# Reordering the first loads, moving the gate arithmetic and waiting directly on row stores in a graph-attention kernel

## What is computed

```
h = relu(layernorm(x))                       # 8192 x 256
e = leaky_relu(h @ a[:256] + (h @ a[256:]).T, 0.2)
U = softmax(where(adj > 0, e, -9e15), axis=1)          # adj is 8192 x 8192
rowsum = sum(U * 0.5 * U, axis=1);  coe = sigmoid(temp)   # temp has 5 entries
feat = soft_threshold(U @ h + (1 - coe[2] - rowsum) * h)
out = x + coe[1] * feat_even2 + (1 - coe[1]) * (coe[0] * feat_odd2 + (1 - coe[0]) * h0)
```

## Time and profile before

| | |
|---|---|
| runs | 1456.39, 1456.82, 1457.94 us (median 1456.82) |
| profiled execution, its span | 1456.3 us |
| median over the span | 0.5 us |
| PE, DVE, ACT, POOL busy over the span | 62, 66, 59, 40% |
| DMA | 427.22 MB, mean 293 GB/s |
| first computation on x (DVE) | at 16.13 us |
| end of the preparation on DVE | at about 117 us |

### The profile page before, as it was taken

One profiled execution on the slowest core, in us unless ns is written; L12 is line 12 of the kernel. 1 busy time (PEld: TensorE's weight loads), 2 busy tenths in 40 slices (PEclk: granted clock), 3 DMA queues, 4 the chain that ended last, 5 costly groups with the idle time before them and its releaser, 6 DMA issues. The chain is left out here.

```text
span 1456.3 us, 27535 instructions
## 1 busy us (share of the span) xinstructions
PE 896.0 (62%) x3370; PEld 529.5 (36%) x3433; DVE 958.6 (66%) x5347; ACT 854.0 (59%) x1817; POOL 588.7 (40%) x644
## 2 busy tenths in 40 slices
PE   0013766777766767666776776776625655666676
PEld 0000244444443434333333433333314444544443
DVE  5887756768888877888888888887750122333444
ACT  3274576778888888888788788887230222121111
POOL 2002515444343233222212222221227777777775
PEclk9975678889999988998788778877656788788899
DMA  4879798789999999999999999997234566677886
GB/s 95 323 258 328 261 408 298 300 339 364 390 381 371 385 370 368 370 381 385 353 367 356 364 370 363 351 378 281 70 110 122 153 173 195 202 212 228 239 260 211
DMA packets 151277, 427.22 MB, mean 293 GB/s; under 512 B 30333, under 2 KB 112907, under 8 KB 134726
## 3 DMA queue, kind: packets, MB, share of 16 engines
q1 hardware_dynamic: 121084, 349.00, 64.5%
q0 software_dynamic: 30160, 77.90, 17.5%
HBM read 401.31 MB, written 33.90 MB: 299 GB/s over the span
## 5 line engine op out<-in xcount | busy, mean ns | idle before, releaser
L299 ACT ACTIVATE SG<-W,ABOVE 128x4096 bf16<-128x4096 f32 x126 | 466.9, 3706 | 64.8 <-DVE cnt L906 59.5
L587 POOL DMA_INDIRECT R<-haug_d,IDS x228 | 230.6, 1012 | 619.6 <-issue 619.6
L311 PE MATMUL TP<-SG,FOLD 128*128 128x512 bf16 x1004 | 308.2, 450 | 69.6 <-ACT SG L299 64.9
L629 ACT ACTIVATE DG<-ident,WSR 128x128 f32<-128x128 f32 x228 | 75.0, 391 | 312.0 <-PE ACC L643 289.6
L1528 DVE SCALAR_TENSOR_TENSOR W<-ACC,SELF,W 128x256 f32<-128x256 f32 x63 | 30.5, 484 | 241.3 <-PE ACC L643 241.2
L311 PEld LDWEIGHTS TP<-SG,FOLD 128*128 128x128 bf16 x1008 | 115.2, 123 | 182.4 <-ACT SG L299 65.9
L638 PE MATMUL ACC<-R,DG 128*128 128x256 f32 x538 | 180.7, 484 | 0.0
L637 PE MATMUL ACC<-XHO,ZB 128*128 128x256 bf16 x127 | 39.9, 314 | 204.3 <-DMA R<-feat_d,IDT 77.7
L638 PEld LDWEIGHTS ACC<-R,DG 128*128 128x128 f32 x538 | 119.6, 238 | 19.7 <-issue 0.3
L587 POOL DMA_INDIRECT R<-feat_d,IDR x115 | 110.3, 959 | 35.0 <-issue 33.8
L587 POOL DMA_INDIRECT W<-feat_d,IDR x113 | 107.5, 952 | 34.4 <-issue 33.2
(11 more groups left out here) (276 smaller groups left out, 2127.2 us busy)
## 6 DMA issues: line engine op xcount, KB each, us to landing
W<-in_adj_dram SPq DMA_DIRECT2D x128, 2048.0 KB, 10.3
haug_d<-R POOLq DMA_DIRECT2D x8, 1056.0 KB, 8.4
HTS<-haug_d SPq DMA_DIRECT2D x64, 132.0 KB
R<-in_x_dram SPq DMA_DIRECT2D x8, 1024.0 KB, 5.9
feat_d<-FTS SPq DMA_DIRECT2D x64, 128.0 KB, 1.7
W<-in_x_dram SPq DMA_DIRECT2D x64, 128.0 KB
W<-in_L_gnn_h_dram SPq DMA_DIRECT2D x64, 128.0 KB
W<-feat_d SPq DMA_DIRECT2D x64, 128.0 KB
```

The costliest lines, as they stand in the source:

```text
L299: nc.scalar.activation(SG[:, u, half(h)], W2[:, u, half(h)], ACT.Sign, scale=2.0 ** 100, bias=ABOVE[:], accum_out=DEG[:, u, h:h + 1]).then ...
L311: nc.tensor.matmul(KP[u], FOLD[:, b], SG[:, u, b * FW:(b + 1) * FW], start=False, stop=False)
L587: pool.indirect_dma_start(out=g[:, k, 0:w], out_offset=None, in_=table, in_offset=bass.IndirectOffsetOnAxis(ap=ids[:, k:k + 1], axis=0), * ...
L629: nc.scalar.mul(DG[:, u, k], ident[:], weights[:, k:k + 1])
```

## The change

The first two loads of x are issued at once, with no permit; a_row, temp_b and SELF follow behind the second. The semaphore of the small loads is split in two, `row_loaded` (DVE waits for it ahead of stats(1)) and `temp_loaded` (ACT waits for it ahead of the Exp). The Exp moves from ACT's first to ACT's last place in the preparation. The five gate instructions move into the next stage, behind `split_f2`. The three SELF instructions move from behind dots(0) to behind dots(2). `h_free` is gone: ACT waits on the semaphore of the store itself, and POOL's loop waits for no landing until both of its last stores.

```
         def prepare_sync(sp):
-            sp.dma_start(SELF[:], adj.rearrange(...)[0:N * N:N + 1]...).then_inc(diag_loaded, 16)
-            sp.dma_start(a_row[:], ...broadcast_to([P, 2 * F])).then_inc(consts_loaded, 16)
-            sp.dma_start(temp_b[:], ...broadcast_to([P, 5])).then_inc(consts_loaded, 16)
             for g in range(NG):
-                sp.wait_ge(x_free[g % 2], g // 2 + 1)
+                at_least(sp, x_free[g % 2], g // 2)
                 sp.dma_start(X[:, g % 2], x_g[g]).then_inc(x_loaded[g % 2], 16)
+                if g == 1:
+                    sp.dma_start(a_row[:], ...).then_inc(row_loaded, 16)
+                    sp.dma_start(temp_b[:], ...).then_inc(temp_loaded, 16)
+                    sp.dma_start(SELF[:], ...).then_inc(diag_loaded, 16)
...
         def prepare_gpsimd(pool):
-            for u in range(2):
-                pool.sem_inc(h_free[u], 1)
             with pool.Fori(0, NG // 2) as q:
                 for u in range(2):
                     pool.wait_ge(h_done[u], q + 1)
                     pool.dma_start(haug_g[...], H[:, u]).then_inc(h_stored[u], 16)
-                for u in range(2):
-                    pool.wait_ge(h_stored[u], 16 * q + 16)
-                    pool.sem_inc(h_free[u], 1)
+            for u in range(2):
+                pool.wait_ge(h_stored[u], 16 * (NG // 2))

         def prepare_scalar(act):
-            act.wait_ge(consts_loaded, 32)
-            nc.scalar.activation(coe[:], temp_b[:], ACT.Exp, scale=-1.0).then_inc(exp_made, 1)
-            for u in range(2):
-                act.sem_inc(x_free[u], 1)
             for g in range(NG):
...
                 act.wait_ge(norm_ready, g + 1)
-                act.wait_ge(h_free[u], g // 2 + 1)
+                at_least(act, h_stored[u], 16 * (g // 2))
...
+            act.wait_ge(temp_loaded, 16)
+            nc.scalar.activation(coe[:], temp_b[:], ACT.Exp, scale=-1.0).then_inc(exp_made, 1)
...
             norm(0)
-            dve.wait_ge(exp_made, 1)
-            step(nc.vector.tensor_scalar_add(one_m[:], coe[:], 1.0))
-            ...
+            dve.wait_ge(row_loaded, 16)
             for g in range(NG):
...
-                if g == 0:
+                if g == 2:
                     own = Steps(dve, self_step, 0, 2)
                     dve.wait_ge(diag_loaded, 16)
...
                 split_f2()
+                gates()          # the five instructions, behind a wait on exp_made
```

More of the change, by code:

```diff
@@ L252, in end @@
                 assert self.k == self.per, self.k
-        consts_loaded = sem("consts_loaded")
+        row_loaded = sem("row_loaded")
+        temp_loaded = sem("temp_loaded")
         ident_made = sem("ident_made")
@@ L265, in adj_preln_kernel @@
         h_stored = [sem(f"h_stored{u}") for u in range(2)]
-        h_free = [sem(f"h_free{u}") for u in range(2)]
         pads_set = sem("pads_set")
@@ L320, in prepare_sync @@
         def prepare_sync(sp):
-            sp.dma_start(SELF[:], adj.rearrange("a b -> (a b)")[0:N * N:N + 1].rearrange("(t p) -> p t", p=P), allow_slow_non_contiguous=True).then_inc(diag_loaded, 16)
-            sp.dma_start(a_row[:], a.rearrange("f one -> one f").broadcast_to([P, 2 * F])).then_inc(consts_loaded, 16)
-            sp.dma_start(temp_b[:], temp.rearrange("(one k) -> one k", one=1).broadcast_to([P, 5])).then_inc(consts_loaded, 16)
             for g in range(NG):
-                sp.wait_ge(x_free[g % 2], g // 2 + 1)
+                at_least(sp, x_free[g % 2], g // 2)
                 sp.dma_start(X[:, g % 2], x_g[g]).then_inc(x_loaded[g % 2], 16)
+                if g == 1:
+                    sp.dma_start(a_row[:], a.rearrange("f one -> one f").broadcast_to([P, 2 * F])).then_inc(row_loaded, 16)
+                    sp.dma_start(temp_b[:], temp.rearrange("(one k) -> one k", one=1).broadcast_to([P, 5])).then_inc(temp_loaded, 16)
+                    sp.dma_start(SELF[:], adj.rearrange("a b -> (a b)")[0:N * N:N + 1].rearrange("(t p) -> p t", p=P), allow_slow_non_contiguous=True).then_inc(diag_loaded, 16)
                 if g in (3, 4):
@@ L416, in prepare_vector @@
         def prepare_vector(dve):
-            step = Steps(dve, prep_step, 0, 4 + 10 * NG)
+            step = Steps(dve, prep_step, 0, 10 * NG)
             def stats(g):
@@ L1063, in body, with gates @@
                         C_.end()
-                top0 = Steps(dve, self_step, 6, 2)
+                top0 = Steps(dve, self_step, 10, 2)
+                def gates():
+                    step = Steps(dve, self_step, 6, 4)
+                    dve.wait_ge(exp_made, 1)
+                    step(nc.vector.tensor_scalar_add(one_m[:], coe[:], 1.0))
+                    step(nc.vector.reciprocal(coe[:], one_m[:]))
+                    step(nc.vector.tensor_scalar(one_m[:], coe[:], -1.0, 1.0, ALU.mult, ALU.add))
+                    nc.vector.tensor_tensor(one_c0[:, 0:1], one_m[:, 1:2], coe[:, 0:1], ALU.mult)
+                    step(nc.vector.tensor_tensor(one_c0[:, 1:2], one_m[:, 1:2], one_m[:, 0:1], ALU.mult))
+                    step.end()
                 def split_f2():
```

## The result

The changed kernel takes 1441.62 us, median of 4 runs (1438.67 to 1443.99), beside 1457.38 us (1456.39 to 1460.58) for the kernel before: ratio 0.9889 [0.9866, 0.9912]. Every ratio here is to runs of the kernel before on the same chip. Repeated beside more runs of the kernel before, the ratio was 0.9874 [0.9848, 0.9899] and 0.9876 [0.9855, 0.9896].

What follows compares the result with a forecast made beforehand. The prediction took DVE's chain in the preparation as the bound: 9.56 us from the head plus 1.8 us from gates and direct waits, 11.4 us in all, gave 1445.4 us, with 8 in 10 for 1442.5 to 1449.5.

Steps and rivals of the forecast that it cites:

- The head: Start of the preparation: x issued first at 0.97, so DVE starts at 6.57 instead of 16.13, 9.56 us off.
- The covers: Slack said to hide moved work: over 2 us for SELF instructions, 1.3 us for Exp, 2.6 us for gates.
- The vanished load: ACT's table load at line 741 in the next stage should vanish: counted as 0, with 1.3 us kept for the range.
- Gates off the head: Five gate instructions, 0.9 us, leave DVE between norm(0) and stats(1): at most 0.2 us gained, at dots(0).
- Direct waits on the stores: Relus in the preparation: about 0.1 us at relu(2), at most 0.1 at relu(4), 1.5 at relu(6); 1.8 with gates.
- the two meet, so 1.8 is also all there is: At dots(6), relu(6)'s end at 99.84 and stats(7)'s at 99.85 in the old clock cap the preparation's gain at 1.8 us.
- The later stages: Stages after the preparation were to keep their lengths within 1 us each.
- Only the head: Rival: store(4) lands later or store(5) did not hold h_free; gain 9.9 us, 1446.9 us; 12 in 100.
- the small loads in the way: Rival: a_row's load or SELF's transfers overlap x, costing 3.9 us on DVE's chain, 1449.3 us; 8 in 100.
- The loop gives it back: Rival: the sparse loop's 63 blocks lengthen, 0.18 us each cancelling the gain; 4 in 100 slower, 4 about as before.
- It doesn't do what it says: Rival: the first x is slow while instructions and first addresses are still fetched, so the head shrinks; no separate chance.
- More than the sum: Rival: the vanished table load counts for 1.3 us or the loop falls better, 1442 to 1444 us; 8 in 100.

Runs made afterwards that it cites:

- after_hfree: The changed kernel with h_free put back, POOL waiting for both landings at each turn's end and telling ACT: 1443.89 us, ratio 0.9911.
- before_x_first: The kernel before with only the loads of x first and without permits, everything else as it was: 1447.05 us, ratio 0.9930.
- before_unrolled: The kernel before with POOL's loop of four turns written out with fixed addresses, h_free and order kept: 1449.95 us, ratio 0.9969.
- relay kernel: The kernel before with h_free kept, but POOL telling of each store's landing before it takes up the next store: 1451.43 us, ratio 0.9971.
- the two on the other chip: The changed kernel with POOL's loop written out, without and with a 0.52 us fill on POOL ahead of stores (0) and (2): ratios 0.9851 and 0.9848.
- written out, with the fill: The changed kernel with POOL's loop written out and a 0.52 us memset on POOL ahead of stores (0) and (2): ratio 0.9848.
- after_again: The changed kernel run once more, unaltered, beside more runs of the kernel before: 1439.46 us, ratio 0.9874.

## Why the prediction was right and wrong

**The head was right.** 9.43 us of 9.56, with x issued at 0.97 and DVE 0.13 us later than said. Every kernel that has x first without SELF ahead shows it: statistics at 6.66 to 6.87, 7.10 with temp_b ahead. The small loads were not in the way: no idle time ahead of stats(1), and the next x, issued at 18.33, landed at 23.72.

**The covers held.** Dots(2) waited 4.76 us ("over 4.5"). The Exp is followed by 1.29 us of idle time, and the wait for PE behind the gates is 2.33 us, where 2.6 was said. Two table loads are left of three (0.97 and 99.74 us; before 0.97, 10.71 and 184.69). The load at 99.74 takes 1.28 us, the Exp starts 0.01 us behind its end and takes 0.21, so the two together are the 1.5 us of the working, and the copy of F2 was not held by them. The vanished load shows where I looked for it and is taken back where I said: 17.84 us of gain when the next Exp starts, 16.35 at the Sign behind it, which now waits 4.27 us for adj. Gates off the head gave 0.19 us for 0.2.

**The step that failed is "Direct waits on the stores".** It had 1.8 us with the gates, and for the waits alone the runs show 5.1 (kernel before) and 4.8 (kernel after). At F2's copy the sum is 3.6 us short, about what the median missed the forecast by (3.8). At relu(6) the working was right: on the landing of store(4), 74.17 + 8.3 = 82.47 against 82.57. At relu(4) the term was 0.1 us, because 61.92 + 11.2 = 73.12 and relu(4) came at 73.23. The wait was read rightly: in both profiles of the kernel before relu(4) stands on store(2)'s landing. What failed is that I carried the 11.2 us into the changed kernel as if they were the store's own. It lands in 8.4 to 9.0 us in all eight profiles with direct waits in the loop.

The second releaser I missed altogether. POOL took up store(3) at 72.23, and the `h_free` increments of the pair stand behind it:

```profile
72.23 0.89 POOL L380 DMA_DIRECT2D haug_d<-R  x1 [9.42 <-DVE F L461]
```

I had named exactly this for store(5) and relu(6), and did not ask it of store(3). In after_hfree, before_x_first and before_unrolled the store was down 1 to 3 us before, and relu(4) still came right behind store(3). The row that bounds the step was there: equal stores took from 9.0 us, and 61.92 + 9.0 is 70.9, 2.3 us ahead of 73.23. I used the landings' scatter to bound relu(6) from below and not relu(4) from above. With it the low end would have been about 1440.

A bound of the same step was wrong too, without harm to the sum: "the two meet, so 1.8 is also all there is" took DVE at dots(6) for the limit. Dots(6) did lose all its idle time, but the chain goes on from relu(6) over ACT to relu(7), and the copy of F2 had relu(6)'s whole gain.

**What it showed in its place.** Relu(4), 12.48 - 10.04 = 2.4 us more than relu(2): by the rows nearly all of it is store(2)'s landing, 8.9 us instead of 11.2. With direct waits POOL takes store(2) up 0.4 us ahead of the next load of x instead of 0.3; whether that tenth is the reason is the question of the table below. With `h_free` only 0.9 us of that could have been had, since relu(4) would then have stood on store(3) at 72.3; the rest needs the order. The relay kernel, with a landing of 9.1 us and relu(4) at 70.63, has both. Relu(6), 2.5 us more: 1.4 is the order that I had, 0.7 the landing in 8.3 us instead of 9.0, and 0.4 that store(4) is taken up 13.42 us behind relu(4) instead of 13.85.

**Relu(2) and its store** were right by luck. Store(0) is taken up at once in after (0.8 us behind its data, before 3.0), but then lands in 13.7 us instead of 11.9: 39.9, where 49.83 less the 9.63 of dots(0) is 40.2. Gain and loss cancel.

**The later stages** were to keep their lengths within 1 us. In the profile one is 6.5 us shorter and one 2.2 longer. But from the copy of F2 to the end the executions of after and its variants lie between 1333.5 and 1339.0 us (the two on the other chip left out), those of before (1338.8, 1337.0) and its variants between 1332.4 and 1339.1. The medians gain 15.8 to 17 us where the preparation gains 15.0 to 15.3. Whether 1 or 2 us of it is real I can't say; nothing that I tried isolates it. Nor does the median of each part follow its step closely: x first 8.8 us for 10.4, the waits 2.7 for 5.1, `h_free` put back 4.4 for 4.8.

**The rivals.** *Only the head* and *the small loads in the way* are out. Requests of SP's queue did overlap in before: from the first x's issue at 10.53 to its landing at 16.03 it moved 234 GB/s, 1.29 MB, where that load is 1.05 MB. But in after a_row, behind both loads of x, landed at 11.0, ahead of stats(1) at 14.12, where DVE waits for it. *The loop gives it back* did not happen; the two levels of the granted clock that it speaks of are 1.00 and 0.50, which 146 of the 160 stretches of 1 us from 300 to 460 us in before show. *It doesn't do what it says* did not happen either: in after x lands 5.6 us behind its issue, in before 5.5, and the instruction queue moved one packet (0.01 MB) in the first 20 us of after. No run shows a first load held up by such fetching. *More than the sum* named the right side and about the right time, 1442 to 1444, for the wrong reason: the table load is taken back by the wait for adj.

## What to carry to other kernels

Let a consumer wait on the transfer it needs, not on an engine that relays it with other work queued in front: here the order held a relu back by 1.0 to 3.8 us each time that its store was down first, and the relay itself cost 0.1 us. When two possible releasers stand within the scatter of one of them, one profile doesn't say which it is; bound the step by the other one as well. Don't carry a transfer's time over to a kernel that issues it at another moment: store(2), 1056 KB each time, took 7.2 to 13.2 us in the 17 profiles here. Put what starts a chain first into the queue (9.43 us here), and a load of thousands of single elements behind it (SELF ahead of x cost 5.4 us).

## What the hardware showed that I had not expected

**Tenths of a microsecond in the issue go with several in the landing.** Each store of 1056 KB meets the next load of x of 1024 KB on the other queue. Its time to land against its lead (issue of that load less take-up of the store):

| store | lead, us | lands in, us | kernels |
|---|---|---|---|
| (0) | load first by 1.85 to 2.2 | 11.5 to 12.0 | `h_free` in the loop |
| (0) | 0.27 | 13.7 to 14.0 | direct waits, loop |
| (0) | 0.56 | 8.8 | written out, with the fill |
| (0) | 0.77 | 6.4 to 6.5 | written out |
| (2) | 0.30 | 9.1 to 13.2 (5 profiles) | `h_free` in the loop |
| (2) | 0.40 to 0.42 | 8.4 to 9.0 (8 profiles) | direct waits, loop |
| (2) | 0.77 to 0.80 | 7.2 to 8.0 (4 profiles) | written out |
| (4) | 0.31 to 0.32 | 8.9 to 9.0 (5 profiles) | `h_free` in the loop |
| (4) | 0.42 to 0.45 | 8.3 to 8.4 (7 profiles) | direct waits, loop |
| (4) | 0.74 | 6.2 | direct waits, loop (after_again) |
| (4) | 0.80 to 0.87 | 6.1 to 6.7 (3 profiles) | written out |
| (4) | 1.51 | 6.0 | written out, fill at (0) and (2) |

The three groups of store(2) do not overlap in 17 profiles. But from group to group the loop's form changes with the lead. In two places the lead varies and the form does not. One is the fill at store(0): 0.77 to 0.56, and 6.4 to 8.8 us. The other is store(4) in two executions of one and the same kernel, after (74.17 in the profile above, 8.3 us) and after_again. The next load of x in after, then load, store and landing in after_again:

```profile
74.59 0.37 SPq L323 DMA_DIRECT2D R<-in_x_dram  x1
```

```profile
74.65 0.37 SPq L323 DMA_DIRECT2D R<-in_x_dram  x1
```

```profile
73.91 0.89 POOL L379 DMA_DIRECT2D haug_d<-R  x1 [10.04 <-DVE F L457]
```

```profile
haug_d<-R POOLq DMA_DIRECT2D x1, 1056.0 KB, 6.2
```

So the loop's form is not needed for the difference. It is one profile each, and the lead is not all: at 0.30 us store(2) still took anything from 9.1 to 13.2. What the two transfers do to each other no run shows.

**POOL took the first store up later in a loop.** Behind its data POOL took up store(0) in 0.32 us when written out, 0.82 in the loop with direct waits, and 2.95 to 3.25 in the loop with `h_free`. The waits aren't it (0.82 with them, telling nobody). Loop and computed address went together in every edit, so which of them costs the 0.5 us isn't separated, and why the loop with the increments costs 2 us more in the first turn alone stays open.

**Single elements.** SELF's 8192 elements of 4 bytes keep the 16 engines 0.90 busy for 5 us. The issue right behind them takes 5.0 to 5.3 us, be it a_row's or x's, and x lands 5.4 us later; issued behind x at 4.16 they land 11.0 us later, at 15.2, and delay nothing that is waited for: the next x, issued at 18.33, lands in 5.4 us.
